# Last stage of a four-part block on one core: the value product as three fp32r terms instead of one fp32 product

## The chip, the core and the metric

The kernel runs on one core of a Trainium2 chip. The metric is the device time of one execution in microseconds (us), the median of several runs.

## What is computed

Four layers stand behind one another, each with a layer norm ahead of it and a residual sum behind it, on x of 4 x 2048 x 256 in fp32: a broadcast value row, a feed-forward layer with a token shift, a banded attention with rotary positions, and the same feed-forward layer again. The change is in that last layer. Cut to what matters:

```python
def ffn(x, W_r, W_k, W_v, mu_r, mu_k):          # x: layer norm of the residual stream
    x_prev = concatenate([zeros, x[:, :-1, :]])  # the token before
    xr = mu_r * x + (1.0 - mu_r) * x_prev
    xk = mu_k * x + (1.0 - mu_k) * x_prev
    r = sigmoid(einsum('btc,dc->btd', xr, W_r))
    k_act = square(relu(einsum('btc,dc->btd', xk, W_k)))
    return r * einsum('btc,dc->btd', k_act, W_v)
x = x + ffn(layernorm(x), ...)
```

## The kernel before

The 8192 tokens lie as 64 blocks of 128. A feed-forward stage takes them in 16 chunks of 4 blocks (512 tokens). `ffn_stage` builds the stage twice: for the first layer (`value` and `weights` given, `past` None) and for the last one (`past` is the attention stage). In between runs the attention stage in 64 steps. Each engine has its own queue, written out by hand as a sequence of `step(c)` calls, and waits on semaphores; `real(c)` drops what lies outside of the 16 chunks.

A chunk c of the last stage goes through these steps. SyncE loads x. VectorE: `moments` (mean and variance). GpSimd: `std_of` (`veps`, then the power, `rstd`, L316 and L319). VectorE: `shift_of` (L397). ScalarE: `normalize`, two parts (L545, it waits for `shift_made`). TensorE: `transposes` (L659). ScalarE: `edge` (L494, only for an even chunk: copies the last token's column) and four `behind_of` (L524), the token before times 1 − mu, for receptance (R) and keys (K) and two channel halves k. VectorE: four `mixed` (L409), the sum with mu times x. ScalarE: `high_of` (L534), an fp32r copy. VectorE: `low_of` (L421), mix minus high. TensorE: `keys_of` (L674), two halves of six matmuls 128x512: three terms (high by high, high by low weights, low by high) times two channel halves; `receptance` (L688), 24 matmuls 128x256 in three terms. ScalarE: `relu_of` (L553) and `square_of` (L562) for each half of the channels, `sigmoid_of` (L568) for each half of the tokens. TensorE: `values` (L706), for each half of the tokens four fp32 matmuls of `act` with `w_v`; the profile shows two passes for each. VectorE: `gate_value` (L430). GpSimd: `add_gated` (L325). SyncE: store.

The orders that matter, in one step c of the last stage. TensorE: values(c-1, 0), keys(c, 0), transposes(c+1, 1), keys(c, 1), transposes(c+1, 0), receptance(c, 1), receptance(c, 0), values(c-1, 1). GpSimd: add_gated(c-2, 1), std_of(c+2), add_gated(c-1, 0). VectorE: low(c, K), gate(c-2, 1), moments(c+2), low(c, R), mixed(c+1, K, 1), gate(c-1, 0), shift(c+2), and three more `mixed(c+1, ...)`. ScalarE is told by the diff below.

The attention stage overlaps with the beginning of the last stage. Its last rows are made by `bias_rows(i)` on GpSimd (L1247, x plus the output bias), `output(i)` on TensorE (L1711) and `residual(i)` on VectorE (L1369). GpSimd's queue holds `std_of(2)` of the last stage ahead of `bias_rows` of the last two rows; VectorE's holds `shift_of(2)` of `opening` ahead of the last two `residual`, and these ahead of step 1 of the last stage. On TensorE values(0, 0) waits for all 64 residual rows (`past.x_made`) and stands ahead of keys(1, 0).

Of the kernel before, what the change touches and what calls it, by code (L numbers as in the profile page):

```python
# [25 lines left out]
P = 128  # L26
# [31 lines left out]
def identity(nc, pool, tile, made, n=1):  # L58
# [13 lines left out]
F = 65536  # L72
# [12 lines left out]
          "gated": PREPARED["raw"]}  # L85
# [16 lines left out]
def ffn_stage(nc, stack, name, x_in, x_out, tiles, place, banks, first=None, weights=None, value=None, side=None,  # L102
# [77 lines left out]
    gated = sb("gated", [P, 2, 2, 2 * C])  # L180
    w_h, w_l, w_v, mu, mu_rest, ident = tiles
# [38 lines left out]
    if value is not None:  # L220
# [10 lines left out]
        va_stats = sem("va_stats")  # L231
        va_mv = sem("va_mv")
        va_veps = sem("va_veps")
        va_rstd = sem("va_rstd")
        va_xn = sem("va_xn")
        va_t = sem("va_t")
        va_xt = sem("va_xt")
# [58 lines left out]
    def gpsimd(pool):  # L296
# [8 lines left out]
        if value is not None:  # L305
            pool.wait_ge(va_mv, 1)
            nc.gpsimd.tensor_tensor(va_stds[:, 0:1], va_mean[:, 1:2], eps[0:BATCH, 0:1], ALU.add).then_inc(va_veps, 1)
            pool.wait_ge(va_veps, 1)
            nc.gpsimd.tensor_tensor(va_stds[:, 1:2], va_stds[:, 0:1], power[0:BATCH, 0:1],
                                    ALU.pow).then_inc(va_rstd, 1)  # L310
# [25 lines left out]
        def step(c):  # L336
# [13 lines left out]
    def vector(dve):  # L350
        need = Need(dve)
        if value is not None:
            dve.wait_ge(value_in, 16)
            nc.vector.bn_stats(va_moments[:, :], va[:, :]).then_inc(va_stats, 1)
            dve.wait_ge(va_stats, 1)
            nc.vector.bn_aggr(va_mean[:, :], va_moments[:, :]).then_inc(va_mv, 1)
            dve.wait_ge(va_rstd, 1)
            nc.vector.tensor_scalar(va[:, :], va[:, :], va_mean[:, 0:1], va_stds[:, 1:2], ALU.subtract,
                                    ALU.mult).then_inc(va_xn, 1)
# [64 lines left out]

        def gate_value(c, h):
# [7 lines left out]
        def step(c):  # L433
# [47 lines left out]
    def scalar(act_e):  # L481
# [21 lines left out]
        if value is not None:  # L503
            edge(0)
            act_e.wait_ge(va_t, 1)
            nc.scalar.activation(mix[:, 0, :, :].rearrange("p k (b t) -> p k b t", b=BATCH),
                                 t_ps[:, :, 0:BATCH].unsqueeze(3).broadcast_to([P, CK, BATCH, P]),
                                 ACT.Copy).then_inc(va_xt, 1)
# [27 lines left out]
        def normalize(c, part):  # L536
            if real(c):
# [4 lines left out]
                if value is not None and c == 0:  # L542
                    act_e.wait_ge(va_t, 1)
# [26 lines left out]
        def step(c):  # L570
# [19 lines left out]
            else:  # L590
# [1374 lines left out]
```

## Time and profile before

| what | value |
|---|---|
| median of 3 runs | 1600.47 us (1599.98 to 1602.84) |
| profiled execution | 1603.56 us |
| its span, first to last instruction | 1601.8 us |
| mean granted TensorE clock | 0.986 |
| busy share of the span | PE 93%, DVE 88%, ACT 83%, POOL 71% |
| TensorE busy from 1460 to 1580 us | 20.00 of every 20 us |

PE is TensorE, DVE VectorE, ACT ScalarE, POOL GpSimd. Busy shares are means over stages with different limits; what a change in one stage is worth is read from that stage, from which wait ends last there. Records of ScalarE and VectorE overlap a little, since an instruction starts before the one ahead of it has written everything. A matmul's end is modelled, so a busy TensorE is not a TensorE at its peak.

### The profile page before, as it was taken

Reading aid. Unit: us, or ns where it says so; the run is one execution under the profiler, and the core shown is the slowest. Engines: PE = TensorE matmul, PEld = TensorE weight load, DVE = VectorE, ACT = ScalarE, POOL = GpSimd, SP = SyncE. Lnnn points to the kernel's source line nnn. Section 1 sums busy time; section 2 is a strip of 40 time slices with the busy share of each in tenths; the row PEclk is TensorE's granted clock in tenths of the full one; section 3 lists DMA queues with packets and bytes.
Section 4 is the critical chain, followed back from the end, with each engine's and each line's share of the span. In section 5 each row is a group of like instructions: output and inputs, shape, how many; then the busy total and the mean of one; then the engine's idle time right before and its main releaser. Section 6 shows DMA issues by size and latency. Waiting matters only on the chain. (4 is left out here: it accounts for less than half of the span.)

```text
span 1601.8 us, 46976 instructions
## 1 busy us (share of the span) xinstructions
PE 1494.2 (93%) x16866; PEld 1144.1 (71%) x16866; DVE 1401.9 (88%) x3859; ACT 1324.2 (83%) x2442; POOL 1139.1 (71%) x911
## 2 busy tenths in 40 slices
PE   5999978899999999999999999999999999889998
PEld 4888745577777677766767776766677777678887
DVE  5999668999999999999999999999999899857885
ACT  5999658888888888888788888888888878759996
POOL 4665267878787887878787878787887777623443
PEclk8999999999999999999999999999999999989999
DMA  5232247999999899999999999999999998962331
GB/s 213 93 125 92 89 79 138 165 177 172 181 178 173 172 166 171 178 175 182 172 168 168 172 181 174 182 173 178 165 171 169 176 165 157 175 161 83 108 108 67
DMA packets 729886, 247.94 MB, mean 155 GB/s; under 512 B 689588, under 2 KB 716472, under 8 KB 729656
## 3 DMA queue, kind: packets, MB, share of 16 engines
q1 hardware_dynamic: 711816, 228.93, 75.4%
q10 hardware_dynamic: 17840, 16.00, 3.8%
q8 instruction: 137, 2.24, 0.6%
q14 instruction: 93, 0.76, 0.2%
HBM read 47.73 MB, written 25.17 MB: 46 GB/s over the span
## 5 line engine op out<-in xcount | busy, mean ns | idle before, releaser
L1471 ACT ACTIVATE at_prob<-at_prob,at_top 128x256 f32<-128x256 f32 (+1 forms) x1024 | 428.3, 490 | 19.2 <-DVE at_top L1307 16.6
L1307 DVE CUSTOM_DVE_ANT_0 at_prob<-banks,at_masks,pre_s_scale 128x256 f32<-128x256 f32 (+1 forms) x1024 | 421.2, 472 | 26.1 <-PE banks L1739 9.4
L1319 DVE TENSOR_TENSOR at_halves<-at_prob,at_halves 128x1024 f16<-128x1024 f32 (+1 forms) x256 | 331.5, 1295 | 3.1 <-ACT at_halves L1480 3.1
L1624 PE MATMUL banks<-at_xt,pre_w_h 128*128 128x512 f16 x1024 | 296.9, 382 | 12.5 <-ACT at_v_l L1499 9.2
L1739 PE MATMUL banks<-at_kt,at_qt 32*128 32x256 f32 (+1 forms) x4096 | 253.1, 383 | 42.5 <-POOL at_qt L1209 19.2
L1739 PEld LDWEIGHTS banks<-at_kt,at_qt 32*128 32x128 f32 x4096 | 198.5, 187 | 104.0 <-issue 99.3
L1480 ACT ACTIVATE at_halves<-at_prob 128x1024 f16<-128x1024 f32 (+1 forms) x256 | 263.4, 1029 | 6.1
L1199 POOL TENSOR_TENSOR at_kt<-at_k_by 128x512 f32<-128x512 f32 x128 | 176.0, 1375 | 65.7 <-DVE at_halves L1319 62.4
L1189 POOL TENSOR_TENSOR at_q_by<-at_q_first,at_tables 128x512 f32<-128x512 f32 x128 | 175.7, 1377 | 61.6 <-DVE at_halves L1319 59.6
L1695 PE MATMUL banks<-at_v_h,at_pt 128*128 128x65 f16 x1984 | 207.9, 195 | 11.0 <-DMA at_pt<-at_halves 9.0
L1695 PEld LDWEIGHTS banks<-at_v_h,at_pt 128*128 128x128 f16 x1984 | 182.0, 97 | 45.5 <-issue 24.5
L1209 POOL TENSOR_TENSOR at_qt<-at_q_by 128x512 f32<-128x512 f32 x128 | 210.4, 1663 | 0.0
L1696 PE MATMUL banks<-at_v_l,at_pt 128*128 128x64 f16 x1984 | 207.6, 193 | 0.0
L1697 PE MATMUL banks<-at_v_h,at_pt 128*128 128x65 f16 x1984 | 207.2, 194 | 0.0
L325 POOL TENSOR_TENSOR f_x<-f_x,f_gated 128x512 f32<-128x512 f32 x64 | 83.1, 1309 | 154.2 <-DVE f_gated L430 154.2
L1696 PEld LDWEIGHTS banks<-at_v_l,at_pt 128*128 128x128 f16 x1984 | 182.2, 99 | 8.7
L1697 PEld LDWEIGHTS banks<-at_v_h,at_pt 128*128 128x128 f16 x1984 | 182.5, 98 | 0.0
L1179 POOL TENSOR_TENSOR at_k_by<-at_k_first,at_tables 128x512 f32<-128x512 f32 x128 | 171.9, 1365 | 2.5 <-ACT at_k_first L1528 2.5
L1528 ACT ACTIVATE at_k_first<-banks,pre_bias 128x512 f32<-128x512 f32 x64 | 44.0, 687 | 155.3 <-PE banks L1624 155.3
L1624 PEld LDWEIGHTS banks<-at_xt,pre_w_h 128*128 128x128 f16 x1024 | 86.8, 98 | 113.9 <-issue 34.6
L1641 PE MATMUL banks<-pre_w_h,at_xt 128*128 128x256 f16 x1024 | 164.1, 273 | 0.9 <-ACT at_q_first L1538 0.8
L1238 POOL TENSOR_TENSOR at_c_halves<-at_ctx,at_c_halves 128x1024 f16<-128x1024 f32 x64 | 137.4, 2147 | 23.4 <-DVE at_halves L1319 13.9
(123 smaller groups left out, 3329.8 us busy)
## 6 DMA issues: line engine op xcount, KB each, us to landing
f_x<-in_x SPq DMA_DIRECT2D x16, 512.0 KB, 3.7
x_after_ffn<-f_x SPq DMA_DIRECT2D x16, 512.0 KB, 2.7
f_x<-x_after_attention SPq DMA_DIRECT2D x16, 512.0 KB, 4.4
out_x<-f_x SPq DMA_DIRECT2D x16, 512.0 KB, 3.0
at_x_res<-x_after_ffn ACTq DMA_DIRECT2D x61, 128.0 KB, 2.6
x_after_attention<-at_x_res ACTq DMA_DIRECT2D x58, 128.0 KB, 2.1
at_x_ln<-x_after_ffn SPq DMA_DIRECT2D x32, 128.0 KB, 2.9
at_tables<-in_cos SPq DMA_DIRECT2D x16, 256.0 KB, 3.6
```

Of the source, the lines that this page charges most:

```text
L1189: nc.gpsimd.tensor_tensor(q_by[:, n, :], q_first[:, :], tables[:, r, n // 3, :], ALU.mult).then_inc(q_made[n], 1)
L1199: nc.gpsimd.tensor_tensor(kt[:, half, own(t, 0):own(t, 0) + SB, :].rearrange("p s t -> p (s t)"), k_by[:, 2 * half, :], k_by[:, 2 * half + ...
L1209: nc.gpsimd.tensor_tensor(qt[:, t % 2, half, :], q_by[:, 2 * half, :], q_by[:, 2 * half + 1, :], (ALU.subtract, ALU.add)[half]).then_inc(q ...
L1307: last = nc.vector.tensor_tensor_reduce(out=prob[:, n % 2, h, low:2 * P], in0=s_ps[:, h, n % 2 * 2 * P + low:(n % 2 + 1) * 2 * P], in1=mas ...
L1319: nc.vector.tensor_tensor(parts[:, 1, :, :], prob[:, n % 2, :, keys_from(t, b):2 * P], parts[:, 0, :, :], ALU.subtract).then_inc(p_low, 1)
L1471: last = nc.scalar.activation(at, at, ACT.Exp, bias=top[:, n % 2, h:h + 1], scale=-1.0)
L1480: nc.scalar.activation(halves_of(n, alone(t, b))[:, 0, :, :], prob[:, n % 2, :, keys_from(t, b):2 * P], ACT.Copy).then_inc(p_high, 1)
L1624: last = nc.tensor.matmul(pr_ps[:, half, :].rearrange("p (b t) -> p b t", b=SB), w[wp][:, k, at:at + P], xt[:, r, :, xp, k, :], start=n == ...
L1695: nc.tensor.matmul(out, ph, v_h[:, at, h, :], start=s == 0, stop=False)
L1696: nc.tensor.matmul(out[:, 0:HD], ph, v_l[:, at, h, :], start=False, stop=False)
L1697: last = nc.tensor.matmul(out, pl, v_h[:, at, h, :], start=False, stop=s == len(slots) - 1)
L1739: last = nc.tensor.matmul(s_ps[:, h, d * 2 * P + keys_from(t, b):(d + 1) * 2 * P] .rearrange("p (s t) -> p s t", t=P), qt[rows_of, par, ha ...
```

## The change

Only for the last stage. `wv_h` and `wv_l` (high and low part of the value weights) are made once: the high part by ScalarE at the start of its `opening`, the low part by VectorE behind `residual(STEPS - 5)`. For each chunk and channel half VectorE copies `act` to fp32r (`act_high_of`), GpSimd subtracts that from `act` (`act_low_of`), and `values` runs three terms: 12 matmuls for each half of the tokens in place of 4 fp32 ones. It now waits for `act_low`. ScalarE's order is changed: the squares come forward between the `behind` copies. In the first stage seven semaphores are replaced by one that counts; no work is changed there.

```diff
@@ gpsimd, last stage
+        def act_low_of(c, m):
+            if real(c):
+                pool.wait_ge(act_high, keyed(c, m))
+                need(v_done, in_turn(c - 2, 1))
+                nc.gpsimd.tensor_tensor(act_l[:, c % 2, m, :], act[:, c % 2, m, :], act_h[:, c % 2, m, :].bitcast(F32),
+                                        ALU.subtract).then_inc(act_low, 1)
@@ step
                 add_gated(c - 2, 1)
                 std_of(c + 2)
+                act_low_of(c, 0)
+                act_low_of(c, 1)
                 add_gated(c - 1, 0)
@@ vector
+        def value_weights_low():
+            dve.wait_ge(wv_high, 1)
+            nc.vector.tensor_tensor(wv_l[:, :, :], w_v[:, :, :], wv_h[:, :, :].bitcast(F32),
+                                    ALU.subtract).then_inc(wv_low, 1)
+
+        def act_high_of(c, m):
+            if real(c):
+                dve.wait_ge(act_made, keyed(c, m))
+                need(v_done, in_turn(c - 2, 1))
+                nc.vector.tensor_copy(act_h[:, c % 2, m, :], act[:, c % 2, m, :]).then_inc(act_high, 1)
@@ step
                 gate_value(c - 2, 1)
                 moments(c + 2)
                 low_of(c, R)
+                act_high_of(c, 0)
                 mixed(c + 1, K, 1)
                 gate_value(c - 1, 0)
+                act_high_of(c, 1)
                 shift_of(c + 2)
@@ opening
             residual(past.STEPS - 5)
+            value_weights_low()
             moments(1)
@@
             for m, k in sorted(MIX_NTH, key=MIX_NTH.get):
                 mixed(1, m, k)
+            act_high_of(0, 0)
+            act_high_of(0, 1)
             shift_of(2)
@@ scalar, step
                 relu_of(c + 1, 0)
                 edge(c + 2)
                 behind_of(c + 2, R, 1)
+                square_of(c + 1, 0)
                 sigmoid_of(c, 0)
                 behind_of(c + 2, K, 1)
                 relu_of(c + 1, 1)
                 behind_of(c + 2, R, 0)
+                square_of(c + 1, 1)
                 behind_of(c + 2, K, 0)
-                square_of(c + 1, 0)
-                square_of(c + 1, 1)
@@ opening
+            act_e.wait_ge(past.q_roped[0], past.STEPS)
+            nc.scalar.activation(wv_h[:, :, :], w_v[:, :, :], ACT.Copy).then_inc(wv_high, 1)
@@ tensor, values
-                pe.wait_ge(act_made, in_turn(c, 1))
+                if past is not None:
+                    pe.wait_ge(act_low, in_turn(c, 1))
+                else:
+                    pe.wait_ge(act_made, in_turn(c, 1))
@@
+                        for n, (wp, xp) in enumerate(TERMS):
+                            for k in range(CK):
+                                last = nc.tensor.matmul(
+                                    v_ps[:, h, j * C:(j + 1) * C], (act_h, act_l)[xp][:, c % 2, k, t:t + P],
+                                    (wv_h, wv_l)[wp][:, k, :], start=n == 0 and k == 0, stop=n == 2 and k == CK - 1)
```

## Rows read from the trace of the kernel before

**Rows 1.** Chain of waits, last stage: start us, length us, engine, tile, line, count.
```profile
1462.82 3.45 PE banks L706 x16
...
1479.91 2.82 PE banks L688 x24
...
1582.26 3.45 PE banks L706 x16
```

**Rows 2.** Timeline of ScalarE: start us, length us, engine, line, operation, tiles, shapes, count.
```profile
1537.37 0.60 ACT L553 ACTIVATE f_relu<-banks 128x512 f32<-128x512 f32 x1 [0.59 <-PE banks L674]
1537.86 0.69 ACT L524 ACTIVATE f_behind<-banks,ffn_mu_rest 128x512 f32<-128x512 f32 x1
1538.43 0.60 ACT L568 ACTIVATE f_gate<-banks 128x512 f32<-128x512 f32 x1
...
1539.96 1.30 ACT L524 ACTIVATE f_behind<-banks,ffn_mu_rest 128x512 f32<-128x512 f32 x2
1541.10 1.20 ACT L562 ACTIVATE f_act<-f_relu 128x512 f32<-128x512 f32 x2
1542.15 1.13 ACT L545 ACTIVATE f_xn<-f_x,f_shift,f_rstd 128x256 f32<-128x256 f32 x2
```

**Rows 3.** Timeline, one step before: normalization, low part, key product.
```profile
1532.29 1.13 ACT L545 ACTIVATE f_xn<-f_x,f_shift,f_rstd 128x256 f32<-128x256 f32 x2
...
1534.40 1.23 DVE L421 TENSOR_TENSOR f_mix_l<-f_mix,f_mix_h 128x1024 fp32r<-128x1024 f32 x1 [0.89 <-ACT f_mix_h L534]
...
1535.68 0.73 PE L674 MATMUL banks<-f_mix_h,ffn_w_h 128*128 128x512 f32 x2
```

**Rows 4.** Timeline where TensorE stood idle ahead of the key product of chunk 2.
```profile
1447.81 0.58 ACT L553 ACTIVATE f_relu<-banks 128x512 f32<-128x512 f32 x1
...
1456.06 0.73 PE L674 MATMUL banks<-f_mix_h,ffn_w_h 128*128 128x512 f32 x2 [0.26 <-DVE f_mix_l L421]
...
1457.75 0.60 ACT L553 ACTIVATE f_relu<-banks 128x512 f32<-128x512 f32 x1 [0.59 <-PE banks L674]
```

**Rows 5.** Groups of VectorE over the span: busy us, mean ns, idle before.
```profile
L1406 DVE COPY at_bv_wide<-at_bv_cols 128x1024 f32<-128x1024 f32 x1 | 0.7, 683 | 0.0
```

**Rows 6.** Timeline of VectorE and GpSimd in the step of rows 2.
```profile
1540.91 0.15 DVE L397 SCALAR_TENSOR_TENSOR f_shift<-f_mv,f_rstd 128x4 f32<-128x4 f32 x1
1541.30 2.07 DVE L409 SCALAR_TENSOR_TENSOR f_mix<-banks,ffn_mu,f_behind 128x512 f32<-128x512 f32 x3 [0.23 <-ACT f_behind L524]
...
1541.08 1.30 POOL L325 TENSOR_TENSOR f_x<-f_x,f_gated 128x512 f32<-128x512 f32 x1 [0.85 <-DVE f_gated L430]
```

**Rows 7.** Timeline, two places where VectorE and GpSimd both use SBUF operands.
```profile
608.14 0.72 POOL L1247 TENSOR_TENSOR at_x_res<-at_x_res,at_out_bias 128x256 f32<-128x256 f32 x1
...
608.15 1.79 DVE L1319 TENSOR_TENSOR at_halves<-at_prob,at_halves 128x1024 f16<-128x1024 f32 x1
...
1447.42 1.02 POOL L319 TENSOR_TENSOR f_rstd<-f_veps,f_power 128x4 f32<-128x4 f32 x1
...
1447.94 1.23 DVE L421 TENSOR_TENSOR f_mix_l<-f_mix,f_mix_h 128x1024 fp32r<-128x1024 f32 x1 [0.88 <-ACT f_mix_h L534]
```

**Rows 8.** Timeline of the opening of the last stage, four engines.
```profile
1437.54 0.72 POOL L1247 TENSOR_TENSOR at_x_res<-at_x_res,at_out_bias 128x256 f32<-128x256 f32 x1 [4.22 <-DMA at_x_res<-x_after_ffn]
...
1439.86 2.07 DVE L409 SCALAR_TENSOR_TENSOR f_mix<-banks,ffn_mu,f_behind 128x512 f32<-128x512 f32 x3 [0.89 <-ACT f_behind L524]
...
1442.59 0.48 DVE L1369 SCALAR_TENSOR_TENSOR at_x_res<-banks,pre_o_down,at_x_res 128x256 f32<-128x256 f32 x1 [0.20 <-PE banks L1711]
...
1443.22 1.96 PE L706 MATMUL banks<-ffn_w_v,f_act 128*128 128x256 f32 x8 [0.67 <-DVE at_x_res L1369]
...
1445.39 0.73 PE L674 MATMUL banks<-f_mix_h,ffn_w_h 128*128 128x512 f32 x2 [0.20 <-DVE f_mix_l L421]
```

**Rows 9.** Stretches, TensorE: from:to, us, busy us (records), granted clock, DMA share, GB/s.
```profile
1406.00:1408.00 2.00, 0.00 (x0) 0.76 1.13 208
1408.00:1413.00 5.00, 4.81 (x41) 0.50 1.01 213
```

More of the change, by code:

```diff
@@ L180, in ffn_stage @@
     gated = sb("gated", [P, 2, 2, 2 * C])
+    if past is not None:
+        act_h = sb("act_h", [P, 2, CK, N], F32R)
+        act_l = sb("act_l", [P, 2, CK, N], F32R)
+        wv_h = sb("wv_h", [P, CK, C], F32R)
+        wv_l = sb("wv_l", [P, CK, C], F32R)
+        wv_high = sem("wv_high")
+        wv_low = sem("wv_low")
+        act_high = sem("act_high")
+        act_low = sem("act_low")
     w_h, w_l, w_v, mu, mu_rest, ident = tiles
@@ L230, in ffn_stage @@
         wa_in = sem("wa_in")
[L231 to L237, printed above, removed]
+        va_chain = sem("va_chain")
+        VA_STATS, VA_MV, VA_VEPS, VA_RSTD, VA_XN, VA_T, VA_XT = range(1, 8)
         va_done = sem("va_done")
@@ L305, in gpsimd @@
         if value is not None:
-            pool.wait_ge(va_mv, 1)
-            nc.gpsimd.tensor_tensor(va_stds[:, 0:1], va_mean[:, 1:2], eps[0:BATCH, 0:1], ALU.add).then_inc(va_veps, 1)
-            pool.wait_ge(va_veps, 1)
+            pool.wait_ge(va_chain, VA_MV)
+            nc.gpsimd.tensor_tensor(va_stds[:, 0:1], va_mean[:, 1:2], eps[0:BATCH, 0:1], ALU.add).then_inc(va_chain, 1)
+            pool.wait_ge(va_chain, VA_VEPS)
             nc.gpsimd.tensor_tensor(va_stds[:, 1:2], va_stds[:, 0:1], power[0:BATCH, 0:1],
-                                    ALU.pow).then_inc(va_rstd, 1)
+                                    ALU.pow).then_inc(va_chain, 1)
         def std_of(c):
@@ L353, in vector @@
             dve.wait_ge(value_in, 16)
[L354 to L357, printed above, removed]
+            nc.vector.bn_stats(va_moments[:, :], va[:, :]).then_inc(va_chain, 1)
+            dve.wait_ge(va_chain, VA_STATS)
+            nc.vector.bn_aggr(va_mean[:, :], va_moments[:, :]).then_inc(va_chain, 1)
+            dve.wait_ge(va_chain, VA_RSTD)
             nc.vector.tensor_scalar(va[:, :], va[:, :], va_mean[:, 0:1], va_stds[:, 1:2], ALU.subtract,
-                                    ALU.mult).then_inc(va_xn, 1)
+                                    ALU.mult).then_inc(va_chain, 1)
         def value_of(b):
@@ L504, in scalar @@
             edge(0)
-            act_e.wait_ge(va_t, 1)
+            act_e.wait_ge(va_chain, VA_T)
             nc.scalar.activation(mix[:, 0, :, :].rearrange("p k (b t) -> p k b t", b=BATCH),
                                  t_ps[:, :, 0:BATCH].unsqueeze(3).broadcast_to([P, CK, BATCH, P]),
-                                 ACT.Copy).then_inc(va_xt, 1)
+                                 ACT.Copy).then_inc(va_chain, 1)
         if weights is not None:
@@ L542, in normalize @@
                 if value is not None and c == 0:
-                    act_e.wait_ge(va_t, 1)
+                    act_e.wait_ge(va_chain, VA_T)
                 for j in (2 * part, 2 * part + 1):
@@ L638, in tensor @@
         if value is not None:
-            pe.wait_ge(va_xn, 1)
+            pe.wait_ge(va_chain, VA_XN)
             for k in range(CK):
                 last = nc.tensor.transpose(t_ps[:, k, 0:BATCH], va[:, k * P:(k + 1) * P], ident[0:BATCH, 0:BATCH])
-            last.then_inc(va_t, 1)
-            pe.wait_ge(va_xt, 1)
+            last.then_inc(va_chain, 1)
+            pe.wait_ge(va_chain, VA_XT)
             pe.wait_ge(wa_in, 32)
@@ L695, in values @@
             if real(c):
-                pe.wait_ge(act_made, in_turn(c, 1))
+                if past is not None:
+                    pe.wait_ge(act_low, in_turn(c, 1))
+                else:
+                    pe.wait_ge(act_made, in_turn(c, 1))
                 need(gated_made, in_turn(c - 1, h))
@@ L700, in values @@
                     pe.wait_ge(past.x_made, past.STEPS)
+                    pe.wait_ge(wv_low, 1)
                 if weights is not None and c == 0:
@@ L704, in values @@
                     t = (2 * h + j) * P
-                    for k in range(CK):
-                        last = nc.tensor.matmul(v_ps[:, h, j * C:(j + 1) * C], act[:, c % 2, k, t:t + P],
-                                                w_v[:, k, :], start=k == 0, stop=k == CK - 1)
+                    if past is not None:
+                        for n, (wp, xp) in enumerate(TERMS):
[3 more added lines that the diff above has]
+                                    (wv_h, wv_l)[wp][:, k, :], start=n == 0 and k == 0, stop=n == 2 and k == CK - 1)
+                    else:
+                        for k in range(CK):
+                            last = nc.tensor.matmul(v_ps[:, h, j * C:(j + 1) * C], act[:, c % 2, k, t:t + P],
+                                                    w_v[:, k, :], start=k == 0, stop=k == CK - 1)
                 last.then_inc(v_done, 1)
```

2 lines of the change are left out of this document (1 added, 1 removed).

## Prediction

> **What bounds the kernel now.** I read the views in the order chain of waits, timeline, waits of one stretch. The change touches the last stage alone (from about 1409 us to the end; some names in the first stage change, no work). In the chain of waits, steps of that stage follow one another on TensorE alone: the value products stand in it at 1462.82 and at 1582.26, twelve steps later, so a step takes 119.44 / 12 = 9.95 us [rows 1]. That looks like a stage bound by TensorE. The reader should see in the timeline that a second loop is as long. I count from the start of the first relu of a chunk, R. ScalarE then runs without a gap: to the first normalization 1542.15 − 1537.37 = 4.78 us [rows 2]; from there to the low part of the mixed keys on VectorE 2.11, to the key product on TensorE 3.39 (1532.29, 1534.40, 1535.68) [rows 3]. From the start of the key product to the next R it is 1.69: 1456.06 to 1457.75, a place where TensorE had stood idle for 0.26 behind VectorE, so that nothing but latency is in it [rows 4]. Sum: 4.78 + 3.39 + 1.69 = 9.86 us. In every second chunk ScalarE also copies the edge column; such a step is R to R in [rows 4], 1457.75 − 1447.81 = 9.94. So the loop relu, normalize, high, low, key product takes 9.90 on average, and TensorE takes 9.95. Whatever is taken from TensorE can give back 0.05 us a step.
>
> **The change part by part.**
>
> *Value product.* Removed: 16 passes in 3.45 us a chunk [rows 1]. Added: 24 fp32r matmuls of the shape of the receptance product, which take 2.82 [rows 1]. TensorE saves 0.63 a chunk; its step would be 9.32. By the loop above only 0.05 of it is seen, until the last chunk: behind the last receptance product nothing is left but three half value products, and these save 1.5 x 0.63 = 0.94 at the end.
>
> *ScalarE's new order.* The squares come forward: the first right behind the first `behind`, the second right behind the third `behind`, and the last `behind` is the one that moves back. ScalarE does the same work until the normalization (4.78). A square takes half of 1542.15 − 1541.10, 0.52 from start to start; relu takes 0.49, a `behind` 0.57, and from sigmoid to the squares there are 2.67 [rows 2]. So the second square starts at R + 0.49 + 0.57 + 0.52 + (2.67 − 0.57) = 3.68, and ends about 4.36 (0.68 long); the last `behind` ends at 4.89.
>
> *The copy of the high part, VectorE.* The trace has no 128x512 copy. It has one of 128x1024 in 0.68 [rows 5], against 1.23 for a subtraction of the same size [rows 3]. If the copy runs at twice the rate, the fixed part is 0.13 and 128x512 takes 0.41; I take 0.42. The ends are 0.34 (half of the row, no fixed part) and 0.68 (one rate for both, should the fp32r output forbid the faster one). The second copy starts 0.04 behind the square, as the mixes do behind `behind` (1539.96 + 1.30 = 1541.26, mixes at 1541.30 [rows 2, 6]): R + 4.40. In VectorE's queue stand behind it `shift_of`, then the mixes. Who waits: `shift` (0.15 [rows 6]) is what the normalization needs. Before, it was over at 1541.06, 1.09 before the normalization. Now it ends at 4.40 + 0.42 − 0.07 + 0.15 = 4.90 (VectorE's records overlap by 0.07), and the normalization starts at 4.94 in place of 4.78: 0.16 a step lost. The three mixes start at 4.93 and end at 7.0, and low parts would follow at 4.94 + 2.11 = 7.05, so mixes are just not late.
>
> *The subtraction of the low part, GpSimd.* The nearest row is the addition of the same shape, 1.30 [rows 6]; a 128x256 addition of 0.72 [rows 7] doubled gives 1.44 as the other end; nothing speaks for less than 1.30. The second one starts 0.08 after the copy (4.82), runs 4.90 to 6.20, and only then comes `add_gated(c - 1, 0)`, which so far ran at R + 3.7 (1541.08 [rows 6]): now 6.15 to 7.45. The low part of the keys on VectorE wants to start at 7.05. [Rows 7] show what that means: a VectorE subtraction with two SBUF inputs that started with a GpSimd addition (608.14 to 608.86) took 1.79 where it takes 1.23 alone. It waited for the overlap of 0.71 less 0.14. Here that makes 7.45 − 7.05 − 0.14 = 0.26 a step. The value product itself is not late: its input is there at R + 6.3, key product + 8.0, and TensorE gets to it at 8.1. TensorE's other waits are filled by the 0.9 us that it now idles a step.
>
> *A step in sum*: 4.94 + 3.39 + 0.26 + 1.69 = 10.28, with the edge copy 10.38, mean 10.33 in place of 9.95: + 0.38. From R of chunk 1 to R of chunk 15 there are 14 steps, the last without normalization and by the same sum 10.26: 13 x 0.38 + 0.31 = + 5.2 us. Ends: without the port wait 14 x 0.12 = + 1.7; with a copy of 0.68 another 0.25 a step, + 8.8.
>
> *Opening.* The copy and the subtraction of the weights lie in gaps: ScalarE waits there several us for the next shift, VectorE over 1 us for a DMA, and what gets late by 1 us feeds transposes that TensorE reaches several us later. That is nothing, 1 us if the cover is gone. But the two activations of chunk 0 block three queues. VectorE copies them behind the mixes, which end at 1439.86 + 2.07 = 1441.93 [rows 8], done at 1442.3 and 1442.65. GpSimd has the two subtractions *ahead* of the last two `bias_rows` of the attention stage, which so far ran long before (the last at 1437.54 [rows 8]). It subtracts until 1445.2 (2 x 1.30, and a short wait for the second copy), adds the two rows in 2 x 0.73, to 1446.6, and only then can VectorE make the last residual row (0.48 [rows 8]): 1447.1 in place of 1443.07. Queued behind it on VectorE: the low part of chunk 1's keys, to 1448.3. On TensorE `values(0, 0)` waits for the same row and takes 1.41: key product of chunk 1 at 1448.5 in place of 1445.39. R of chunk 1 is then 1450.2 in place of 1447.81: + 2.4. TensorE stands still from 1442.55 to 1447.1. In [rows 9] it stood still for the 2 us from 1406; the granted clock was 0.76 in them and 0.50, the lower level of 1.2 GHz, in the 5 us behind. The value and first key products are 2.8 us of work, so half speed costs 2.8 at most; I take 1.7, since part of the slow time may pass while TensorE still stands, with 0 and 2.8 as the ends. Opening: + 4.1, ends + 2.4 and + 5.2.
>
> *Sum*: 4.1 + 5.2 − 0.9 = + 8.4 us. The profiled execution took 1603.56 us, span 1601.8, so it would be 1612.0; it lies 3.1 above the median of the runs shown, and the rows of a step repeat to 0.1. I add the same 8.4 to the median: 1600.5 + 8.4 = **1608.9 us**.
>
> **A rule of the skill against the change.** In the trace a VectorE subtraction that started at 1447.94, in the middle of GpSimd's `rstd` (1447.42, 1.02 long), took 1.23, as alone [rows 7]: so a power over four elements does not hold VectorE back. By the Trainium skill, page "SBUF — State Buffer", section "SBUF: two separate sides", a GpSimd instruction that starts first keeps the shared ports for its whole length; with 608.15 the trace agrees, with 1447.94 it does not. Rival 4 takes the rule at its word.
>
> **The rivals.**
> 1. *TensorE remains the only limit* (faster). The step falls to 9.32: 14 x (−0.63) − 0.9, and + 2.4 of the opening: −7.3, 1593.2 us. It decides once the loop over ScalarE is under 9.32. For it speaks the chain; against it [rows 4], where that loop ran with TensorE idle and took 9.94. Chance 0.06.
> 2. *Copy and subtraction are covered* (no change). If normalization and low part keep their places, the step is 9.90: −0.7 − 0.9 + 4.1 = + 2.5, 1603.0 us. It would need the shift to be made ahead of the square's copy or the port wait to fall on another pair. Chance 0.14.
> 3. *The copy takes the price of a subtraction*, 0.68: 4.1 + 8.8 − 0.9 = + 12.0, 1612.5 us. Chance 0.12.
> 4. *`rstd` holds the port*: the first copy, ready at R + 1.8, waits until `rstd` ends at 2.87, the chain mix, gate, second copy gets 0.13 later, as does the normalization: another 1.8 us, 1610.7 us. Chance 0.08.
>
> That the change does not do what it says is no rival: the receptance product has the very form of the new matmuls.
>
> **How the numbers follow.** My own sum has 0.60. Slower by over 0.2% (3.2 us, about what a measurement of this kernel can tell from no change) are my sum but for its lowest corner (no clock fall and no port wait: + 3.2), rival 3 and rival 4: 0.78. Within it: rival 2 and that corner, 0.16. Faster: 0.06. The range goes from rival 2 (1603.0, rounded down to 1602.7) to rival 3 with the long clock fall and a slow subtraction, 1614; it leaves out rival 1 and sums of several bad ends.
>
> **What would show it.** Steps right: value products in 24 matmuls of 2.8 us a chunk; TensorE idle some 0.9 us a step ahead of the key product, released by VectorE's low part; ScalarE's normalization released by `shift`; a step of 10.3; a VectorE low part of the keys of about 1.5 us in place of 1.23; relu of chunk 1 some 4 us later and the clock at 0.5 before it. Wrong: copies of 0.7, a step of 9.9 or less, `bias_rows` still ahead of 1440. The prediction is wrong on the whole if the port wait falls on the GpSimd side, or if the clock stays up.

## The result, and the profile after

The changed kernel takes 1609.24 us, median of 5 runs (1607.61 to 1612.19); the kernel before took 1600.47 in 5 runs (1599.8 to 1602.84). The ratio is 1.0051, 95% interval 1.004 to 1.0061: slower by half a per cent. The profiled execution of the changed kernel took 1612.19 us with a span of 1610.4, 8.6 above the span before.

In the changed kernel ScalarE's relu, square, sigmoid and normalization are L582, L591, L597 and L574, its high part L563; VectorE's mixes, low part, copy, shift and gating product L422, L434, L447, L410 and L454; GpSimd's subtraction, addition and bias rows L336, L329 and L1289; TensorE's keys and value product L705 and L743.

One step, the timeline (start us, length us, engine, line, operation, tiles, shapes, count; in brackets what ended an idle time), answering to [rows 2, 3, 6]. Four engines one after the other:

```profile
1534.75 0.60 ACT L582 ACTIVATE f_relu<-banks 128x512 f32<-128x512 f32 x1 [0.92 <-PE banks L705]
...
1539.76 1.10 ACT L574 ACTIVATE f_xn<-f_x,f_shift,f_rstd 128x256 f32<-128x256 f32 x2
...
1545.12 0.60 ACT L582 ACTIVATE f_relu<-banks 128x512 f32<-128x512 f32 x1 [0.89 <-PE banks L705]
...
1539.22 0.43 DVE L447 CAST f_act_h<-f_act 128x512 fp32r<-128x512 f32 x1 [0.23 <-ACT f_act L591]
1539.56 0.16 DVE L410 SCALAR_TENSOR_TENSOR f_shift<-f_mv,f_rstd 128x4 f32<-128x4 f32 x1
1539.80 2.07 DVE L422 SCALAR_TENSOR_TENSOR f_mix<-banks,ffn_mu,f_behind 128x512 f32<-128x512 f32 x3
1541.84 1.52 DVE L434 TENSOR_TENSOR f_mix_l<-f_mix,f_mix_h 128x1024 fp32r<-128x1024 f32 x1
...
1539.73 1.30 POOL L336 TENSOR_TENSOR f_act_l<-f_act,f_act_h 128x512 fp32r<-128x512 f32 x1 [0.88 <-DVE f_act_h L447]
1540.98 1.30 POOL L329 TENSOR_TENSOR f_x<-f_x,f_gated 128x512 f32<-128x512 f32 x1
...
1543.42 0.73 PE L705 MATMUL banks<-f_mix_h,ffn_w_h 128*128 128x512 f32 x2 [0.65 <-DVE f_mix_l L434]
```

Relu to relu is 1545.12 − 1534.75 = 10.37 us; the step next to it, without the edge copy, is 10.28 (first relus of the chunks, to 1555.40). The second copy ends, the shift comes right behind it, the normalization 0.04 behind that: R + 5.01 in this step with the edge copy. The addition lies from 1540.98 to 1542.28 across the start of the low part, which takes 1.52 in place of 1.23, and TensorE stands still for 0.65 until it is done. Over the loop this is what the waits add up to (us in total, times, longest; 1462 to 1590 us):

```profile
ACT f_relu L582 <- PE banks L705: 11.7, 13, 0.9
...
PE banks L705 <- DVE f_mix_l L434: 7.8, 12, 0.7
```

The kernel before had TensorE without a gap there. The page says the same in its chain of the work that ended last, which is now shared; the first line is the kernel before, the second the changed one:

```profile
PE 21%; issue 1%; DVE 1%; ACT 1%; DMA 1%; POOL 0%; SPq 0%; POOLq 0%; DVEq 0%; ACTq 0%
...
PE 15%; DVE 4%; issue 3%; ACT 3%; DMA 1%; POOL 0%; DVEq 0%; POOLq 0%; ACTq 0%; SPq 0%
```

The opening of the stage, answering to [rows 8]:

```profile
1439.36 2.07 DVE L422 SCALAR_TENSOR_TENSOR f_mix<-banks,ffn_mu,f_behind 128x512 f32<-128x512 f32 x3 [0.90 <-ACT f_behind L553]
1441.35 0.75 DVE L447 CAST f_act_h<-f_act 128x512 fp32r<-128x512 f32 x2
1442.01 1.22 DVE L410 SCALAR_TENSOR_TENSOR f_shift<-f_mv,f_rstd 128x4 f32<-128x4 f32 x1
1445.23 0.48 DVE L1411 SCALAR_TENSOR_TENSOR at_x_res<-banks,pre_o_down,at_x_res 128x256 f32<-128x256 f32 x1 [1.99 <-POOL at_x_res L1289]
...
1441.85 2.60 POOL L336 TENSOR_TENSOR f_act_l<-f_act,f_act_h 128x512 fp32r<-128x512 f32 x2 [9.75 <-DVE f_act_h L447]
1444.40 1.40 POOL L1289 TENSOR_TENSOR at_x_res<-at_x_res,at_out_bias 128x256 f32<-128x256 f32 x2
...
1446.65 0.77 PE L743 MATMUL banks<-f_wv_h,f_act_h 128*128 128x256 f32 x2 [4.59 <-DVE at_x_res L1411]
...
1452.15 0.60 ACT L582 ACTIVATE f_relu<-banks 128x512 f32<-128x512 f32 x1 [3.00 <-PE banks L705]
```

and TensorE in stretches of 2 us (from:to, us, busy us, records, granted clock, DMA share, GB/s), answering to [rows 9]:

```profile
1442.00:1444.00 2.00, 0.06 (x1) 1.00 0.00 0
1444.00:1446.00 2.00, 0.00 (x0) 0.80 0.00 0
1446.00:1448.00 2.00, 1.35 (x6) 0.50 0.39 131
1448.00:1450.00 2.00, 2.00 (x10) 0.50 0.00 0
1450.00:1452.00 2.00, 2.00 (x6) 0.50 0.03 8
1452.00:1454.00 2.00, 2.00 (x13) 1.00 0.00 0
```

The stretches add up. The attention stage's end moves by some us from execution to execution, so the opening is counted from the start of the three mixes to the first relu of chunk 1.

| stretch | before | after | difference | forecast |
|---|---|---|---|---|
| three mixes to first relu of chunk 1 | 7.95 | 12.79 | +4.84 | +4.1 |
| that relu to the one of chunk 15, 14 steps | 139.34 | 144.53 | +5.19 | +5.2 |
| from there to the end of the span | 14.65 | 13.72 | −0.93 | −0.9 |
| up to the three mixes | 1439.86 | 1439.36 | −0.50 | 0 |

The sum is 8.60.

### The profile page after: what moved, and what is told of

Same layout as the page of the kernel before. It is cut to its first block and busy times, and to the rows that moved or that the text cites. A ratio compares the mean times of both kernels' runs of the same rounds, so it can differ in the third digit from the quotient of the medians.

```text
span 1610.4 us, 47356 instructions
## 1 busy us (share of the span) xinstructions
PE 1492.2 (93%) x16994; PEld 1146.9 (71%) x16994; DVE 1425.3 (89%) x3892; ACT 1326.3 (82%) x2443; POOL 1180.9 (73%) x943
## 5 line engine op out<-in xcount | busy, mean ns | idle before, releaser
L1241 POOL TENSOR_TENSOR at_kt<-at_k_by 128x512 f32<-128x512 f32 x128 | 171.6, 1341 | 64.2 <-DVE at_halves L1361 60.9
L1251 POOL TENSOR_TENSOR at_qt<-at_q_by 128x512 f32<-128x512 f32 x128 | 214.1, 1692 | 0.0
L329 POOL TENSOR_TENSOR f_x<-f_x,f_gated 128x512 f32<-128x512 f32 x64 | 83.0, 1307 | 103.7 <-DVE f_gated L454 103.5
```

What stands on the lines that cost most here:

```text
L1251: nc.gpsimd.tensor_tensor(qt[:, t % 2, half, :], q_by[:, 2 * half, :], q_by[:, 2 * half + 1, :], (ALU.subtract, ALU.add)[half]).then_inc(q ...
```

## The experiments

Steps in this section are counted from the second relu of a chunk to that of the next, in the profile. Each ratio is to the kernel before on the same chip; its median was 1602.26 us beside experiments 1, 2, 4 and 5, 1602.31 beside 3, 7, 8 and 9, 1601.89 beside 6 and 10, and 1602.00 beside 11. The expectations were worked out from 1600.5, so a time is best compared by its ratio. All edits are to the changed kernel unless it is said otherwise.

**1. The value product made cheap, with none of the copies and subtractions (one_term).** The kernel before with an fp32r product in place of the fp32 one, in one term of the three; the two low terms are left out of the computation.

```diff
+        act_e.wait_ge(past.q_roped[0], past.STEPS)
+        nc.scalar.activation(wv_h[:, :, :], w_v[:, :, :], ACT.Copy).then_inc(wv_high, 1)
@@ values: act is written as fp32r by the square
-                                                w_v[:, k, :], start=k == 0, stop=k == CK - 1)
+                                                (w_v if past is None else wv_h)[:, k, :], start=k == 0, stop=k == CK - 1)
```

> The kernel before, with the value product of the last stage as one fp32r term (high by high; the two low terms are left out, so the product is less exact). It takes 2.5 us of work per chunk from TensorE and adds nothing to VectorE and GpSimd. Theory (a loop over relu, normalize, high, low and key product is as long as TensorE's work): a step goes from 9.95 to 9.90 us (9.86 and 9.94 in turn), TensorE idles, 14 steps give 0.7 us; the end behind the last receptance product is about 2.2 us shorter: 1597.6 us. Rival (TensorE is the only limit): a step falls to what ScalarE needs, 9.24 us: 14 x 0.7 + 2.2 = 12 us less, 1588.4 us.

Measured: 1603.12 us, ratio 1.0005 (0.9995 to 1.0015). The mechanism held: eight of the fourteen steps took 9.82 to 9.96 and the last, which has no normalization, 8.19. TensorE was idle for some 2 us in each, waiting for VectorE's low part:

```profile
1538.81 0.73 PE L679 MATMUL banks<-f_mix_h,ffn_w_h 128*128 128x512 f32 x2 [2.08 <-DVE f_mix_l L424]
```

The size did not. The other five steps (the first, second, fourth, eighth and twelfth) took 11.15 to 11.39, and in them the granted clock had fallen (0.50 from 1466 to 1468 us), the key product running at 1.05 us for two matmuls where 0.63 is usual:

```profile
1465.43 0.78 PE L679 MATMUL banks<-f_mix_h,ffn_w_h 128*128 128x512 f32 x2 [1.85 <-DVE f_mix_l L424]
1466.01 1.05 PE L679 MATMUL banks<-f_mix_h,ffn_w_l 128*128 128x512 f32 x2
1466.87 1.05 PE L679 MATMUL banks<-f_mix_l,ffn_w_h 128*128 128x512 f32 x2
```

So with TensorE waiting the loop over ScalarE and VectorE takes 9.9, as the sum of [rows 2 to 4] has it, and rival 1 is dead for this order: a cheaper product alone, at no cost elsewhere, gives next to nothing in the loop. At the end of the span it gave about the 2.2 us that were expected (12.36 from the last chunk's first relu to the end, 14.65 before); the five slow steps took more than that back. What the forecast of this run missed is this fall of the clock, in a loop in which TensorE is idle for 2 us a step; that the idle time is its cause is read from this one kernel, and no run isolates it.

**2. The addition ahead of the second subtraction (add_before).**

```diff
                 act_low_of(c, 0)
-                act_low_of(c, 1)
                 add_gated(c - 1, 0)
+                act_low_of(c, 1)
```

> The changed kernel, with GpSimd's add_gated(c-1, 0) ahead of the second subtraction instead of behind it, in the last stage. Theory (VectorE's low part of the keys waits for the shared port while GpSimd adds): the subtraction of the low part of the keys takes 1.22 again in place of 1.52, the second act subtraction ends near R + 6.8 and the value product is half a us later, which TensorE's idle time takes up; a step goes from 10.33 to 10.05 us: 14 x 0.28 = 3.9 less, 1605.3 us. Rival (the 1.52 has another cause): 1.52 stays, 1609.2 us.

A miss on both sides: 1620.6 us, ratio 1.012 (1.0105 to 1.0135), steps of 10.96 and 11.11. The low part of the keys was back at 1.23, as the theory had it, but the addition had moved beside the copy:

```profile
1541.71 1.28 POOL L329 TENSOR_TENSOR f_x<-f_x,f_gated 128x512 f32<-128x512 f32 x1
...
1541.81 1.47 DVE L447 CAST f_act_h<-f_act 128x512 fp32r<-128x512 f32 x1 [0.23 <-ACT f_act L591]
1543.19 0.15 DVE L410 SCALAR_TENSOR_TENSOR f_shift<-f_mv,f_rstd 128x4 f32<-128x4 f32 x1
...
1543.38 1.09 ACT L574 ACTIVATE f_xn<-f_x,f_shift,f_rstd 128x256 f32<-128x256 f32 x2 [1.03 <-DVE f_shift L410]
```

The copy takes 1.47 in place of 0.43, and shift and normalization come 1.03 late. A copy with one SBUF input and an fp32r output waits for a GpSimd addition as a subtraction does. That the copy of the changed kernel is 0.43 hangs on its place: GpSimd happens to be idle there.

**3. The addition behind the low part (add_after).**

```diff
                 act_low_of(c, 1)
+                if 1 <= c < CHUNKS - 1:
+                    pool.wait_ge(low_made, done(c + 1, MATRIX_NTH[K], 2))
                 add_gated(c - 1, 0)
```

> The changed kernel, with GpSimd's add_gated(c-1, 0) held back by a wait until VectorE has made the low part of the next chunk's keys (from step 1 on). Theory (a VectorE instruction with two SBUF operands waits for the overlap with GpSimd's addition, less 0.14): that low part takes 1.22 instead of 1.52, the second act copy stays at 0.43 since nothing is added beside it, the addition now meets the low part of the receptance, which has room; a step is 10.07 instead of 10.33: 14 x 0.26 = 3.7 us less, 1605.5 us. Rival (GpSimd's subtractions themselves are what is late): no change, 1609.2 us.

Measured: 1606.48 us, ratio 1.0026 (1.0015 to 1.0036), steps of 9.97 and 10.07. The low part of the keys takes 1.23 again. The addition meets the low part of the receptance, for which TensorE is not waiting:

```profile
1538.52 1.23 DVE L436 TENSOR_TENSOR f_mix_l<-f_mix,f_mix_h 128x1024 fp32r<-128x1024 f32 x1
...
1541.99 1.45 DVE L436 TENSOR_TENSOR f_mix_l<-f_mix,f_mix_h 128x1024 fp32r<-128x1024 f32 x1
```

The 14 steps took 139.18 in place of 143.44 (second relus, by which the steps of all experiments are counted), 4.26 less: the wait of the low part for GpSimd's addition is 0.30 of the 0.37 that the change adds to a step. Of the 0.07 that are left, ScalarE's new order alone makes 0.03 (experiment 7).

**4. The shift ahead of the second copy (shift_first).**

```diff
                 gate_value(c - 1, 0)
-                act_high_of(c, 1)
                 shift_of(c + 2)
+                act_high_of(c, 1)
                 mixed(c + 1, K, 0)
```

> The changed kernel, with shift_of ahead of the second copy on VectorE in each step. Theory (the low part of the keys ends a fixed time after GpSimd's addition, whenever it is asked for): the normalization starts 0.16 earlier, the low part starts up to 0.1 earlier and waits that much longer for the port, the step stays at 10.33: 1609.2 us. Rival (the late shift is what costs 0.16 a step by itself, as the sum of the prediction has it): step 10.17, 2.3 us less, 1607.0 us.

Measured: 1610.74 us, ratio 1.0054 (1.0039 to 1.0069), steps of 10.27 and 10.37: no change. The normalization came 0.14 earlier (2.14 behind the second relu in place of 2.28), the low part of the keys began 0.06 earlier (4.30 behind it in place of 4.36), and took 0.06 longer:

```profile
1540.81 1.58 DVE L434 TENSOR_TENSOR f_mix_l<-f_mix,f_mix_h 128x1024 fp32r<-128x1024 f32 x1
```

It ends with the addition either way. The addition began 3.5 us behind the second relu in both kernels. So while it lies there, it alone sets the step, and the shift's delay is inside of it, not beside it.

**5. The bias rows ahead of the first subtractions (rows_first).**

```diff
                 std_of(c + 2)
+                if c == 0:
+                    rows()
                 act_low_of(c, 0)
```

`rows` issues the last `bias_rows` of the attention stage, which so far came behind this step.

> The changed kernel, with GpSimd's last two bias_rows of the attention stage ahead of the first two act subtractions instead of behind them. Theory: the last residual row is made near 1444.3 in place of 1446.4 (span time), TensorE stands still for 2.4 us instead of 4.6, the first relu of chunk 1 starts at 1449.1 to 1449.6 in place of 1452.15 and then waits for ScalarE's own queue: about 3 us less, 1606.2 us. Rival (the opening is covered by something else, the loss is all in the steps): no change, 1609.2 us. The steps stay at 10.33.

Measured: 1606.98 us, ratio 1.0036 (1.0022 to 1.0049). From the mixes to the first relu it is 9.69 in place of 12.79, and the steps are the same. TensorE now stands still for 2.43 us, and its clock stays up. The first relu is no longer held back by TensorE: it waited 3.00 us for it in the changed kernel, and here it starts right behind ScalarE's own work, which the late shift had delayed. TensorE in stretches:

```profile
1438.00:1440.00 2.00, 0.83 (x8) 1.00 0.00 0
1440.00:1442.00 2.00, 0.74 (x6) 1.00 0.32 108
1442.00:1444.00 2.00, 1.54 (x11) 1.00 0.10 32
1444.00:1446.00 2.00, 2.00 (x12) 1.00 0.00 0
```

**6. TensorE kept busy in the gap (warm_gap).**

```diff
             if real(c):
+                if past is not None and c == 0 and h == 0:
+                    pe.wait_ge(relu_made, 2)
+                    for _ in range(18):
+                        nc.tensor.matmul(k_ps[:, 0, :], w_h[:, WK, 0, 0:P], mix_h[:, 0, K, 0, :], start=True, stop=True)
                 if past is not None:
                     pe.wait_ge(act_low, in_turn(c, 1))
```

> The changed kernel with 18 idle matmuls of 128x512 put ahead of values(0,0): TensorE multiplies into the key bank while it waits for the first subtractions, and the product is never read. My theory: the opening lost part of its 4.84 us to TensorE's clock (0.50 from 1446 to 1452, through all of the first value product and the first half of the next keys). Kept busy, the engine keeps 1.00: values(0,0) takes 1.4 instead of 2.8 us and the key half ahead of the first relu 1.4 instead of 2.3, so the first relu of the loop comes 2 to 2.4 us earlier and the time is about 1607 us. The steps stay at 10.33. Rival: the opening is late only because the subtractions and bias rows are, and the clock falls all the same: 1609.2 us, no change.

In the profile the theory holds to 0.1: the 18 matmuls fill the gap, the clock stays at 1.00, the value product takes 1.5 in place of 2.7, and from the mixes (1437.53) to the first relu it is 10.48 in place of 12.79, 2.31 less, with the start of the value product where it was (7.37 behind the mixes, 7.29 in the changed kernel).

```profile
1439.98 4.46 PE L730 MATMUL banks<-f_mix_h,ffn_w_h 128*128 128x512 f32 x18
1444.90 0.47 PE L747 MATMUL banks<-f_wv_h,f_act_h 128*128 128x256 f32 x2 [0.46 <-DVE at_x_res L1415]
...
1446.40 0.63 PE L705 MATMUL banks<-f_mix_h,ffn_w_h 128*128 128x512 f32 x2
...
1448.01 0.60 ACT L582 ACTIVATE f_relu<-banks 128x512 f32<-128x512 f32 x1 [0.65 <-PE banks L705]
```

The times don't confirm it: 1609.21 us, ratio 1.0048 (1.0034 to 1.0063), where the changed kernel had 1.0051 (1.004 to 1.0061). The 2.3 us are 0.0014, about as much as either interval reaches to a side, and the three mixes alone started anywhere from 1436.1 to 1441.1 us in the profiled executions of these kernels, which all have the same attention stage. The 2.3 are read from the profile, and stay a single reading. Where they lie is plain from the rows, though: the same first value product and first key half take 2.70 and 2.56 us at 0.50 in the changed kernel, 1.50 and 1.41 here.

**7. The new order of ScalarE alone (order_only).** The kernel before, with the squares where the change puts them.

```diff
                 behind_of(c + 2, R, 1)
+                square_of(c + 1, 0)
                 sigmoid_of(c, 0)
@@
                 behind_of(c + 2, R, 0)
+                square_of(c + 1, 1)
                 behind_of(c + 2, K, 0)
-                square_of(c + 1, 0)
-                square_of(c + 1, 1)
```

> The kernel before, with nothing but ScalarE's new order of the squares in the last stage. Theory (the last behind ends 0.95 later, so the three mixes end at R + 7.0 and hold back the low part of the keys by up to 0.1): a step goes from 9.95 to 10.01 us: + 0.9 us, 1601.4 us. Rival (the order has slack everywhere): 9.95, 1600.5 us.

Measured: 1602.83 us, ratio 1.0006 (0.9997 to 1.0016), steps of 9.91 and 10.06 against 9.86 and 10.04 before, the 14 steps 138.67 against 138.54. The new order costs 0.01 a step over all 14, or 0.03 over the 13 that have a normalization, less than the expected 0.06, and 0.4 at most of the 8.6.

**8. Three edits together (all_three).** The edits of add_after and rows_first, and `shift_of(2)` of the opening ahead of the two copies.

> The changed kernel, with three moves: the addition held back as in add_after, the last two bias_rows ahead of the first act subtractions, and in the opening shift_of(2) ahead of the two act copies on VectorE. Theory: steps of 10.07, first relu of chunk 1 at 8.1 us behind the start of the last three mixes of the opening (7.95 before, 12.8 in the changed kernel), the end 0.9 shorter than before: 1609.2 - 3.7 - 4.6 = 1600.9 us, the same as the kernel before. Rival (the three terms cost by themselves, wherever the waits stand): 1605 us or more.

Measured: 1603.98 us, ratio 1.0006 (0.9997 to 1.0016); from the mixes to the first relu 8.33, steps of 9.97 and 10.07. By its ratio it can't be told from the kernel before, as expected; the time is above the expected 1600.9 mostly because the kernel before took 1602.31 on this chip. By the profile 0.4 in the opening and 0.9 in the loop (first relus: 140.27 in place of 139.34) are left, against the 0.9 saved at the end. In the opening the third edit is all that sets it apart from rows_first, and it is worth 1.36 there (9.69 to 8.33): with the copies first, as in the changed kernel at 1442.01, the shift takes 1.22 for four elements a partition, beside GpSimd's first subtraction, and ScalarE's normalization waits for it.

**9. Everything one step later (one_later).** The step is bound by the loop relu, normalize, high, low, key product. This version takes copies and squares off it (the two copies of the opening go, too, and the diff is cut to the orders): ScalarE makes the high part of the keys first and the squares last, VectorE copies, and GpSimd subtracts, the activations of the chunk before, and gating products and additions come a step later.

```diff
@@ gpsimd
-                add_gated(c - 2, 1)
+                act_low_of(c - 1, 0)
+                act_low_of(c - 1, 1)
                 std_of(c + 2)
-                act_low_of(c, 0)
-                act_low_of(c, 1)
-                add_gated(c - 1, 0)
+                add_gated(c - 2, 0)
+                add_gated(c - 2, 1)
@@ vector
+                act_high_of(c - 1, 0)
+                act_high_of(c - 1, 1)
+                gate_value(c - 2, 0)
                 gate_value(c - 2, 1)
                 moments(c + 2)
                 low_of(c, R)
-                act_high_of(c, 0)
                 mixed(c + 1, K, 1)
-                gate_value(c - 1, 0)
-                act_high_of(c, 1)
-                shift_of(c + 2)
                 mixed(c + 1, K, 0)
+                shift_of(c + 2)
                 mixed(c + 1, R, 0)
@@ scalar; both squares go to the end of the step, behind_of(c + 2, K, 0) ahead of behind_of(c + 2, R, 0)
-                normalize(c + 2, 0)
                 high_of(c + 1, K)
+                normalize(c + 2, 0)
@@ tensor
-            values(c - 1, 0)
                 keys_of(c, 0)
...
                 transposes(c + 1, 0)
+                values(c - 1, 0)
                 receptance(c, 1)
```

> The changed kernel, built so that the loop is short: ScalarE makes the high part of the keys ahead of the normalization, the squares stand last again, copies, subtractions, gates and additions of a chunk run one step later (behind the low part of the next chunk's keys), and TensorE's first half value product stands behind the transposes of the step. Theory (with the loop at 9.0 us TensorE's saving is seen): the low part of the keys ends near R + 7.2, a step falls to TensorE's 9.32 to 9.5 us; opening as in the kernel before; end 0.9 shorter or, with the later act chain, equal: 1592 to 1595 us. Rival (VectorE, with 8.9 us of work in a step, and the port become the limit): 9.9 us or more a step, 1600 us or more.

A miss: 1619.22 us, ratio 1.0104 (1.0089 to 1.0119). The first two steps took 9.11 and 9.52, about as expected, then eleven took 11.36 to 11.80. Two new waits had come up:

```profile
1538.17 1.41 DVE L398 BATCH_NORM_STATS2 f_stats<-f_x 128x6 f32<-128x256 f32 x4 [1.81 <-DMA f_x<-x_after_attention]
...
1542.34 1.21 DVE L410 SCALAR_TENSOR_TENSOR f_shift<-f_mv,f_rstd 128x4 f32<-128x4 f32 x1
```

The moments wait 1.8 for x: SyncE issues the load of x(c+4) behind the store of x(c-1), and that store now waits for an addition one step later. And the shift takes 1.21, beside the first of the two additions.

**10. Without those two waits (one_later_2).** Both edits were made together, so what each wait cost by itself isn't shown.

```diff
@@ sync
-                store(c - 1)
-                fetch(c + AHEAD)
+            fetch(c + AHEAD)
+            store(c - 1)
@@ gpsimd
+                if 2 <= c < CHUNKS - 2:
+                    pool.wait_ge(shift_made, c + 3)
                 add_gated(c - 2, 0)
                 add_gated(c - 2, 1)
```

> The version of one_later with its two waits taken out: SyncE issues the load of x(c+4) ahead of the store of x(c-1) instead of behind it, and GpSimd starts its two additions only when VectorE's shift of that step is made. My theory: one_later had the right work in the right places, and lost its gain to x arriving 2.0 us late at the moments and to the shift waiting 1.1 for the additions. Without these the steps are those that its first two showed, 9.1 to 9.5 us, TensorE with almost no idle time: 1450.3 for the first relu, 14 x 9.4, 13.9 to the end and 1.8 around the span make 1597.6 us, 3 below the kernel before (1595 to 1600). Rival: the step is bounded by a chain through ScalarE and VectorE which those two waits only hid; it then stays over 9.9 and the time at 1605 or more.

Measured: 1598.74 us, ratio 0.9978 (0.9967 to 0.9988), faster than the kernel before. Most steps are 9.65 and 9.80, a little over the expected 9.4. The cause stands on VectorE and GpSimd: the additions, held back for the shift, now meet the low part of the next keys and the two copies of the next step. The wait goes both ways. The low part started 0.03 ahead of the second addition (1510.22) and took its usual 1.22, and that addition took 2.33 in place of 1.30; the first copy, which then met the addition, took 1.52 in place of 0.42.

```profile
1508.96 3.59 POOL L325 TENSOR_TENSOR f_x<-f_x,f_gated 128x512 f32<-128x512 f32 x2 [0.31 <-DVE f_shift L408]
...
1510.19 1.22 DVE L432 TENSOR_TENSOR f_mix_l<-f_mix,f_mix_h 128x1024 fp32r<-128x1024 f32 x1
1511.32 1.86 DVE L445 CAST f_act_h<-f_act 128x512 fp32r<-128x512 f32 x2
```

**11. The gating product ahead of the copies (one_later_3).**

```diff
+                gate_value(c - 2, 0)
                 act_high_of(c - 1, 0)
                 act_high_of(c - 1, 1)
-                gate_value(c - 2, 0)
```

> The version of one_later_2 with VectorE's gate_value(c-2,0) moved ahead of its two copies. In one_later_2 the copies came while GpSimd's additions were still running and took 1.86 instead of 0.75 us, so the low part of the receptance was made 0.2 late for TensorE and the subtractions 0.14 late for the value product: 0.35 of a step of 9.72. My theory: the gating product reads its first operand from PSUM and does not wait for the additions, so it fills that wait; the moments, the shift and the additions then come about 0.5 earlier, both waits of TensorE go, and the step is 9.4 to 9.5: 14 x 0.25 = 3.5 us less, 1595.5 us. Rival: the copies end only when the additions do, and nothing behind them comes earlier: 1598.7 us, no change.

Measured: 1595.78 us, ratio 0.9965 (0.9951 to 0.9979), in the later part of the loop steps of 9.26 and 9.65 in place of 9.65 and 9.80; the 14 steps took 132.13 in place of 135.23. The product takes its usual 0.68 beside the addition and fills the time in which the copies would wait; they take 1.25 in place of 1.86:

```profile
1506.76 0.68 DVE L452 TENSOR_TENSOR f_gated<-banks,f_gate 128x512 f32<-128x512 f32 x1
1507.36 1.25 DVE L445 CAST f_act_h<-f_act 128x512 fp32r<-128x512 f32 x2
```

The change pays in this order. The 13 steps with a normalization take 9.41 in the mean, 9.95 in the kernel before: 0.54 of TensorE's 0.63 is seen once the copies and squares are off the loop and the shift is made clear of the additions. It is the fastest version of all that ran.

## Why the prediction was right

Forecast 1608.9 us, measured 1609.24, in the range from 1602.7 to 1614.0. Point by point:

- *The second loop* (9.90 beside TensorE's 9.95): right. one_term, where its clock is up, has steps of 9.82 to 9.96 with TensorE idle for 2 us in each.
- *A step of 10.28 and 10.38, + 0.38 a step*: 10.29 and 10.36 from first relu to first relu, + 5.19 us over the loop where 5.2 were forecast. The parts: the copy takes 0.43 (mean 0.435 of 25; taken as 0.42); the normalization starts at R + 5.01 in a step with the edge copy (4.94 + 0.10); the subtraction takes 1.296 in the mean (1.30); the low part waits 0.30 (0.26), which is the overlap with the addition, 1542.28 − 1541.84 = 0.44, less 0.14, as [rows 7] gave it. TensorE is idle for 0.65 in a step, less than the 0.9 named as a sign. The split into 0.16 for the late shift and 0.26 for the port reads as two costs side by side, and they are not. The wait was taken as the addition's end less the low part's start, so in the sum itself the place of the normalization drops out: had the shift been on time, the same sum would have given a wait of 0.42 and the same 10.28. shift_first shows just that. With the addition moved off instead (add_after), a step is 0.07 longer than before, where the sum without the port wait has 0.12, and 0.03 of that is ScalarE's order.
- *The opening, + 4.1*: measured + 4.84, the term that was mis-sized. The queue was read rightly: the bias rows behind both subtractions, the residual rows behind these. With the clock kept up (warm_gap) the first relu comes 10.48 behind the mixes, + 2.53 where 2.4 were forecast. The clock cost 2.3 (the same single profile) where 1.7 was taken. That 1.7 was a choice between the ends of 0 and 2.8, not a reading, and that it fell within 0.6 is luck. The clock fell late in the gap (1.00 from 1442 to 1444, 0.80 from 1444 to 1446), so that most of the slow time passed while TensorE worked: it was at 0.50 through the whole first value product and the first key half. One delay was overlooked: the shift behind the copies waits 1.1 for the first subtraction, and ScalarE's normalization with it. In the changed kernel it costs nothing, since ScalarE is then idle for 3.00 ahead of the first relu, waiting for TensorE. It comes to light once the bias rows are moved: rows_first takes 3.1 off, and the shift's new place another 1.36.
- *The end, − 0.9*: − 0.93.
- *Rival 1* (TensorE the only limit): fallen by one_term and by TensorE's 0.65 of idle time in each step. Only another order comes near it: one_later_3, with steps of 9.41 for its 9.32.
- *Rival 2* (copy and subtraction covered): fallen. The nearest to it, made by hand, is add_after: the port wait falls on another pair and the opening costs what it costs in the changed kernel. Its steps are 9.97 and 10.07 for the 9.90 of the rival, and it is 4.2 us above the kernel before for the rival's 2.5. (all_three is no such case: its opening is mended as well.) Of the two things that the rival said it would need, the shift ahead of the copy gave nothing (shift_first); the port wait moved to another pair gave 0.30 a step.
- *Rival 3* (a copy at 0.68): fallen, 0.43. The copy with fp32r output runs at the faster rate that the 128x1024 one of [rows 5] showed.
- *Rival 4* (`rstd` holds the port): fallen. The first copy of a step started 0.03 behind `rstd` and took 0.45, about what it takes alone; when it started 0.10 ahead of it, in the step next to this (1526.18 and 1526.28), the copy took 0.43 and it was `rstd` that took longer (1.21):

```profile
1536.55 1.02 POOL L323 TENSOR_TENSOR f_rstd<-f_veps,f_power 128x4 f32<-128x4 f32 x1
...
1536.58 0.45 DVE L447 CAST f_act_h<-f_act 128x512 fp32r<-128x512 f32 x1 [0.16 <-ACT f_act L591]
```

  Where the larger instructions meet, the rule of the Trainium skill, page "SBUF — State Buffer", section "SBUF: two separate sides", that the one that starts first has the shared ports for its whole length and the other waits, agrees with the traces, but for the 0.14 by which the wait is shorter than the overlap: 1.47 for a copy of 0.43 in add_before, 1.52 for a low part of 1.23, and the other way round 2.33 for an addition of 1.30 in one_later_2. For an `rstd` that starts first it does not agree, as it did not in [rows 7]; an `rstd` that starts second does wait. What bore on this kernel was not the length of `rstd`, but which large GpSimd instruction lies across which VectorE instruction.

## What to carry to other kernels

When the chain of waits shows one engine, look for a second loop in the timeline before giving that engine less work: here it was 0.05 us shorter, and what the change put onto it was lost but for these 0.05. A VectorE instruction on SBUF operands and the GpSimd instruction beside it are a pair to be placed on purpose: write down, for each large GpSimd instruction, what VectorE does meanwhile, and put there what reads one operand from PSUM (the three mixes took 2.07 beside a subtraction, as before, and the gating product 0.68 beside an addition) or what nobody waits for. Work that only feeds a product one step away belongs behind the loop that sets the step; and then look at the loads that stand behind its store in the same queue (one_later: 1.8 us a step).

## What the runs showed of the hardware that was not expected

- A VectorE instruction on four elements a partition waits for a GpSimd instruction as a large one does: the shift takes 0.15 to 0.16 alone and 1.21 to 1.25 when a subtraction or addition of 1.30 to 1.40 had started 0.1 to 0.2 ahead of it. Small instructions in a chain are the ones that pay most for a bad neighbour.
- A VectorE copy with one input (128x512, fp32 to fp32r) takes 0.43 alone, and 1.47 when an addition of GpSimd started 0.10 ahead of it.
- The wait goes the other way as well: a GpSimd addition of 1.30 took 2.33 when a VectorE subtraction of 1.22 had started 0.03 ahead of it (one_later_2).
- TensorE's clock stayed at its upper level in the changed kernel's loop, with 0.65 us of idle time a step, and fell in five of fourteen steps of one_term, with 2.0 us a step; in the openings it stayed up through the gap of 2.43 in rows_first and fell in the one of 4.59 us in the changed kernel. In one_term, where work was taken off TensorE, what was left on it ran slower for a part of the time (1.05 in place of 0.63 for two key matmuls).
